# A second staging buffer for the q and k stores of the projection passes

## The reference, cut to what matters

```python
x = x + attn_a(layernorm(x))   # one head of width 1024, causal, projections q, k, v, o
x = x + ffn(layernorm(x))      # 1024 -> 64, a 16-wide ReLU per column, -> 1024
x = x + attn_b(layernorm(x))   # 16 heads of width 64, causal, Wo, residual, layernorm
x = x + ffn(layernorm(x))
```

```python
q = jnp.einsum('oi,bsi->bso', w_q, in_features)
k = jnp.einsum('oi,bsi->bso', w_k, in_features)
v = jnp.einsum('oi,bsi->bso', w_v, in_features)
...
scores = jnp.where(causal[None, :, :], scores, -jnp.inf)
att = jax.nn.softmax(scores, axis=-1)
```

## Time and profile before

| | us |
|---|---|
| median of the timed runs (2) | 5581.13 |
| the two runs | 5549.98 and 5612.27 |
| the profiled execution | 5427.69 |
| span of its slowest core (core 1), on which all rows below stand | 5425.9 |
| spans of the eight cores | 5402.2 to 5425.9 |
| granted TensorE clock of the eight cores, mean over the span | 0.778 to 0.782 |

### The profile page before, as it was taken

One profiled execution on the slowest core, in us unless ns is written; L12 is line 12 of the kernel. 1 busy time (PEld: TensorE's weight loads), 2 busy tenths in 40 slices (PEclk: granted clock), 3 DMA queues, 4 the chain that ended last, 5 costly groups with the idle time before them and its releaser, 6 DMA issues.

```text
span 5425.9 us, 45860 instructions; the slowest of 8 cores (5402.2 to 5425.9 us)
## 1 busy us (share of the span) xinstructions
PE 3375.0 (62%) x14380; PEld 1272.7 (23%) x14380; DVE 1683.1 (31%) x3093; ACT 1948.8 (36%) x2677; POOL 521.4 (10%) x916
## 2 busy tenths in 40 slices
PE   1257667566777846666645565566766767767762
PEld 1022222234444512222211111111111111121210
DVE  3222121243222142433214443333233232232226
ACT  0012222222222212222233344454655646647660
POOL 1100000000000000100021211111111101101010
PEclk9978888777887867888856676767778777778885
DMA  8633332111111023333210010101101110110100
GB/s 204 183 104 115 119 109 102 62 59 59 40 39 40 16 99 127 103 115 117 77 50 20 24 40 27 44 29 39 37 16 38 41 38 22 38 39 17 41 16 29
DMA packets 219359, 343.27 MB, mean 63 GB/s; under 512 B 88755, under 2 KB 119475, under 8 KB 219126
## 3 DMA queue, kind: packets, MB, share of 16 engines
q1 hardware_dynamic: 140198, 242.80, 13.7%
q0 software_dynamic: 25552, 80.76, 4.4%
q10 hardware_dynamic: 53376, 16.78, 1.3%
HBM read 260.60 MB, written 75.50 MB: 62 GB/s over the span
## 4 chain that ended last, share of the span: by engine, by line
PE 34%; ACT 19%; DVE 18%; DMA 14%; issue 11%; POOL 3%; DVEq 1%; ACTq 0%; SPq 0%; POOLq 0%
ACT arena_b L1265 9%; PE pc L723 5%; PE pc L1235 4%; DMA q_scr<-arena_b 4%; ACT k_sb L1265 4%; PE psQ L1067 4%; PE psQ L683 3%; PE psQ L1258 3%; POOL arena_b L1274 2%; PE pc L1057 2%; PE psQ L1310 2%; DVE stat L810 2%; PE psQ L1315 2%; DMA k_scr<-arena_b 2%; ACT arena_b L690 1%
## 5 line engine op out<-in xcount | busy, mean ns | idle before, releaser
L1265 ACT ACTIVATE arena_b<-psQ,negC 128x1024 bf16<-128x1024 f32 x792 | 865.7, 1156 | 450.5 <-PE psQ L1258 399.4
L683 PE MATMUL psQ<-arena_b 128*128 128x512 bf16 x2048 | 574.6, 434 | 266.9 <-ACT arena_b L699 175.1
L1235 PE MATMUL pc<-arena_b,v_sb 128*65 128x512 bf16 x1584 | 550.8, 433 | 101.0 <-POOL arena_b L1274 100.4
L1258 PE MATMUL psQ<-arena_b 64*128 64x512 bf16 x1528 | 343.0, 439 | 300.6 <-ACT arena_b L1265 199.7
L1321 DVE COPY arena_f<-psQ 64x512 f32<-64x512 f32 x64 | 43.7, 683 | 1387.8 <-PE psQ L1310 1387.8
L1265 ACT ACTIVATE k_sb<-psQ,negC 128x1024 bf16<-128x1024 f32 x360 | 418.4, 1162 | 19.5 <-PE psQ L1258 19.4
L683 PEld LDWEIGHTS psQ<-arena_b 128*128 128x128 bf16 x2048 | 204.5, 107 | 592.3 <-issue 451.3
L1067 PE MATMUL psQ<-arena_b,k_sb 128*128 128x256 bf16 x2176 | 313.8, 292 | 8.8 <-DMA arena_f<-x 8.8
L1274 POOL TENSOR_SCALAR_AFFINE_SELECT arena_b<-arena_b 128x512 bf16<-128x512 bf16 x352 | 207.4, 616 | 1134.4 <-ACT arena_b L1265 1129.4
L723 PE MATMUL pc<-arena_b 128*128 128x512 bf16 x1024 | 252.4, 412 | 101.5 <-DMA arena_b<-wvT_s 52.6
L531 DVE TENSOR_REDUCE nmax<-psQ 1x1 f32<-1x512 f32 x144 | 97.8, 679 | 613.7 <-PE psQ L664 334.9
(11 more groups left out here) (170 smaller groups left out, 4165.7 us busy)
## 6 DMA issues: line engine op xcount, KB each, us to landing
arena_f<-x SPq DMA_DIRECT2D x64, 512.0 KB, 7.1
arena_f<-xs SPq DMA_DIRECT2D x64, 512.0 KB, 5.4
arena_b<-wkT_s SPq DMA_DIRECT2D x16, 1024.0 KB, 8.1
arena_b<-wqT_s SPq DMA_DIRECT2D x16, 1024.0 KB, 7.1
arena_b<-wvT_s SPq DMA_DIRECT2D x16, 1024.0 KB, 7.4
q_scr<-arena_b POOLq DMA_DIRECT2D x128, 128.0 KB, 2.1
xs<-arena_f POOLq DMA_DIRECT2D x32, 512.0 KB, 3.8
arena_b<-wkB_s SPq DMA_DIRECT2D x16, 1024.0 KB, 8.2
```

Of the source, the lines that this page charges most:

```text
L683: p.op("tensor", lambda e_, b=bank, ws=wslot, dc=dc, ec=ec: e_.matmul(b.ap()[:, :], wbuf[:, ws, dc % 4, ec * 128:(ec + 1) * 128], lnxT[:, ...
L1235: p.op("tensor", lambda e_, hh=hh, kc=kc, h=h, att=att, pos=pos, kcnt=kcnt: e_.matmul(pb[4 + hh].ap()[0:65, :], v_sbB[:, kc, h, :], att, s ...
L1258: p.op("tensor", lambda e_, b=bank, hh=hh, ks=kslots[ksl], koff=koff, pr=pr: e_.matmul(b.ap()[:, :], ks[hh * 64:(hh + 1) * 64, koff:koff + ...
L1265: p.op("scalar", lambda e_, ap=AP2[pos % 3], half=half: e_.activation(ap[:, :, :], psQ.ap()[:, half * 1024:(half + 1) * 1024], AF.Exp, bia ...
```

## The change

Staging gets a second buffer, `qstage2`, 1 KB in each partition at offset 16 KB of the float arena. In the stages `phase_a` nothing else uses that place. Even groups go on using `qstage` and the semaphores `s_stq0` and `s_stk0`; odd groups use `qstage2`, `s_stq1` and `s_stk1`. So the copy of group `ec` waits for the landing of the store of group `ec - 2`, where it waited for that of `ec - 1`. The matmuls, the activations, the number and size of the DMAs, the engine that issues them and the order of every stream stay.

```diff
+    qstage2 = af[:, 16 * 256:16 * 256 + 256].bitcast(BF16)
...
                         if staged:
-                            p.wait("scalar", stq_sems[0])
-                            p.wait("scalar", stk_sems[0])
-                            dest = qstage[:, 0, :]
+                            p.wait("scalar", stq_sems[ec % 2])
+                            p.wait("scalar", stk_sems[ec % 2])
+                            dest = qstage[:, 0, :] if ec % 2 == 0 else qstage2
...
                             dma("gpsimd",
                                 dscr[ec, :, tc * TOKC:(tc + 1) * TOKC],
-                                qstage[:, 0, :], stsems[0])
+                                dest, stsems[ec % 2])
```

## The result

| | us |
|---|---|
| changed kernel, median of 11 runs | 5443.92 (5282.80 to 5495.72) |
| kernel before, median of 10 runs | 5520.61 (5434.18 to 5612.27) |
| ratio, 95% interval | 0.9737 (0.9651 to 0.9823) |
| predicted | 5395 (5240 to 5490), a ratio of 0.9667 |

What follows compares the result with a forecast made beforehand. The prediction took the wait for each store's landing, through ACT's copy, to bound the staged passes. Terms of 66 and 115 us gave 181 us off the profiled 5427.7, scaled from the 5581.1 median to 5395 us, range 5240 to 5490.

Steps and rivals of the forecast that it cites:

- The bound and the new wait: Staged passes: the store loop of about 3.3 us sets the groups; with two buffers its wait ends within 4.28 us.
- Landings with two in flight: Staged passes: a store landing takes 2.1 us with two in flight, at worst 4.2 us.
- Rival A: Staged passes: two stores in flight slow landings to 4.2 us, groups 2.7 us apart, 100 us gained, 5478; chance 0.08.
- Term 1: Eight k passes of the second phase: from 233.38 us towards the first phase's 165.23, 66 us gained.
- Term 2: Sixteen q passes: 8.4 us gained each at full clock, 6.0 in about half, mean 7.2, 115 us in all.
- Nothing given back: Outside the staged passes: v passes, attention stages and preparation have no such store and do not change.
- my sign of being wrong: Staged groups staying over 2.7 us apart, or coming down while the sixteen v passes grow.
- Rival C: Other waits, for v weights or next-chunk DVE work, take back two thirds; 60 us left, 5520; chance 0.06.
- Rival B: Denser staged passes: granted clock loses a fifth, groups about 2.6 us, 115 us gained, 5463; chance 0.05.
- The sum: Whole kernel: 66 + 115 = 181 us gained, 3.3% of the profiled 5427.7 us; scaled from 5581.1 to 5395.
- Rival D: Staged passes: colliding stores land in over 5.4 us; at 8 us groups take 4.6 us, 5716, slower; chance 0.03.

Runs made afterwards that it cites:

- four: Changed kernel with four staging buffers and a semaphore each instead of two; ratio 0.9683 to the kernel before, die 1 at 5261.8 us.
- all3_one: all3 with one staging buffer, as in the kernel before; ratio 0.9698 to the kernel before, die 0 at 5254.1 us.
- two_again: Changed kernel run once more without edit, for a second profile; ratio 0.9749 to the kernel before, die 1 at 5267.3 us.
- all3: Changed kernel with slots4's and lazymax's edits, and the next chunk's statistics moved behind the q pass; ratio 0.9304, die 0 at 5047.6 us.
- lazymax: Changed kernel with second-phase group maxima kept in separate columns and joined only at the pass end; die 1 at 5245.4 us, no ratio given.
- gate: Changed kernel without the wait of a pass's first group for the previous pass's last DVE reduction; die 1 at 5264.1 us, no ratio given.
- slots4: Changed kernel with a fourth slot for weight halves, qstage2 moved; ratio 0.9487 to the kernel before, die 1 at 5135.5 us.

## Why the prediction was right, and where its size was off

**The bound and the new wait: right.** The store was the loop. With the second buffer its wait ends before it is needed (5.9 us left of 394.7), and TensorE sets 2.14 us a group. four shows that more buffers bring about 10 us at most; all3_one shows the same wait come back in full when the second buffer goes.

**Landings with two in flight: right in effect, but little tested.** I had asked how long a landing takes with two stores in flight and took 2.1 us. At 2.14 us a group the loop itself hardly has two in flight. Where it has, in the pairs 0.97 us apart, the second landed in 2.8 us (median) in two_again and in 2.2 us in most pairs of all3. So having two in flight does not by itself cost anything, and what delays the second in two_again is not shown. Even 2.8 us fits: 1.13 + 2.8 = 3.9 us is under the 4.28 of two groups. Rival A, 4.2 us and groups 2.7 us apart, fell.

**Term 1, 66 us, measured 52.4.** The step that was off is the sentence that the second phase "also reduces each norm on DVE, which has 7.5 us of work in such a pass of 29 us, so it hides". In the middle of a pass it does. At its end three chains of 1.27 us follow each other while nothing else is there to hide them. The time from the last group to the q pass was 3.9 us before and is 3.9 after; in the first phase, from which I took the target, it is 2.5. Eight times 1.4 us are 11 of the 14 us missing, and lazymax, which shortens exactly this chain, gave 11.4. The other 3 are waits for a store: I took off 2 us for them, and they were 4.7.

**Term 2, 115 us, measured 96.7.** The same step failed again: I booked 1.6 us for the shorter tail in all 16 q passes. In the first phase it came on core 1: from the last group to the v pass it was 9.5 us a pass and is 7.9. In the second it was 8.5 and is 8.6, since the norm matmul of group 7 left one wait and met DVE's. That is 13 to 14 of the 18 us missing. The other part is the third group: I took half of the q passes to find full clock there, and in two_again seven of eight in each phase take 2.6 to 3.6 us for it instead of 1.89. Per pass I had booked 5.6 us for the groups (the mean of 6.8 and 4.4). They gave 4.8 in the first phase and 5.9 in the second, 4 to 5 us less in all.

**Nothing given back: right.** On core 1 the v passes are 4.2 and 2.5 us longer for eight, and growing v passes were my sign of being wrong. But the k passes of the first phase are 4.5 us shorter, and the v passes of one and the same kernel differ by as much from core to core (in two_again 173 to 179 us in the first phase, before 175 to 176). Rival C, with its 121 us, fell, and with it the fear that the loads would take the gain.

**Rival B, the clock.** The staged groups of two_again run at the full clock:

```profile
526.50:535.00 8.50, 8.50 (x37) 3.11 (x36) 0.00 (x0) 4.34 (x8) 1.68 (x4) 1.00 0.17 62
```

In another execution of the same kernel a dense stretch reads 0.81 and groups are 2.56 us apart (last section), near the 2.6 us of rival B. The kernel before also has executions with a lower mean clock (0.72 to 0.75 on a die), so no run shows that the change brings it or makes it more frequent.

**The sum.** 181 forecast, 150 on die 1. By its place in the passes the DVE chain at their ends is 24 of the 31 missing us; taking it away, in lazymax, returned 18 on the passes and 22 on die 1, since a later start of TensorE alone costs nothing (gate). The ratio of 0.9667 that I forecast lies inside the measured interval. That the time lies near is partly luck: I scaled 5581 us, the median of two executions, and ten gave 5521. From 5521 the same gain leads to 5337, further from the measured 5444. Rival D fell: groups come 2.14 us apart and not 4.6. Its 5716 was also not scaled as the others were; scaled it would be 5720.

## What to carry to other kernels

Where one buffer makes producer and store take turns, compare the whole loop (copy, issue, landing, release) with the consumer's period: with n buffers the wait is gone once n periods exceed the loop, and here two were enough (4.28 us against 3.3). A pass without the store that stands beside one with it gives the gain almost for free, but only for the middle: subtract the ends one by one, and ask of each which engine releases it after the first wait is gone. A wait that ends last at one place (TensorE's gate on DVE, the q pass's second weight half) is worth nothing while another chain arrives at the next step at the same time; gate and slots4's q passes show both.

## What was not expected of the hardware

A pause costs more than its length. In slots4 the v passes became up to 36 us shorter for sixteen, beside the waits removed, because they began at 2.4 GHz (granted clock 1.00) instead of 1.2 (0.50). In two_again TensorE did only the norm matmuls in the 7.1 to 8.9 us before each of them, in slots4 in the 1.5 to 2.1 us before.

The dense stretch of a k pass of the first phase stands at a granted clock of 1.00 in the earlier trace rows and in two_again. In the first profile of the changed kernel the same kind of stretch reads:

```profile
590.00:601.00 11.00, 11.00 (x40) 3.71 (x39) 0.00 (x0) 4.65 (x9) 0.00 (x0) 0.81 0.07 26
```

There the groups are 2.56 us apart instead of 2.14. A k pass of the first phase has no store, so the change does not touch it. The Trainium skill, "TensorE: Matmul & The Clock Gate", Part 1, "Seeing it yourself", tells of a limit at 13/16 once three cores of a die run dense matmuls; I had written that the trace disagrees. This row agrees with it, and two_again, with the same kernel on all eight cores, does not show it in these stages. So the limit comes in some executions and not in others; what decides between them is not shown, and they may have run on different chips.
